# The edge stage of a graph attention as one block, its wide lookups in three pairs of PSUM banks, and its first step and key decoding placed earlier

## The reference, cut to what matters

```python
def _forward(x, edge_index, W_gat, att_src, att_dst, b_gat, ...):
    h = (x_flat @ W_gat).reshape(M, HEADS, NUM_EXPERTS)      # 4 heads, 4 experts
    loops = jnp.arange(M)
    src = jnp.concatenate([edge_index[0], loops])            # 524288 edges
    dst = jnp.concatenate([edge_index[1], loops])
    a_src, a_dst = (h * att_src).sum(-1), (h * att_dst).sum(-1)
    e = jax.nn.leaky_relu(a_src[src] + a_dst[dst], negative_slope=0.2)
    e_max = jax.ops.segment_max(e, dst, num_segments=M)
    ee = jnp.exp(e - e_max[dst])
    denom = jax.ops.segment_sum(ee, dst, num_segments=M)
    alpha = ee / (denom[dst] + 1e-16)
    msg = h[src] * alpha[:, :, None]
    agg = jax.ops.segment_sum(msg, dst, num_segments=M).reshape(M, 16) + b_gat
```

## Time and profile before

| what | us |
|---|---|
| median of 3 runs | 1919.39 |
| the runs | 1917.76 to 1920.73 |
| the profiled execution, its own time | 1920.45 |
| its span | 1918.7 |
| start of the table block's work (VectorE L1036) | 705.72 |
| first tail lookup selected (L1433) | 736.56 |
| first block of the main loop (L1345) | 838.41 |
| end of the main loop | 1226 |

### The profile page before, as it was taken

How to read it: one execution, slowest core, us unless ns; L and a number is a source line. 1 busy time by engine, 2 the same in 40 slices (tenths; PEclk the granted TensorE clock), 3 DMA queues, 4 the chain that set the end, 5 groups by cost and what they waited for, 6 DMA issues and landing times. The chain is left out here.

```text
span 1918.7 us, 32883 instructions
## 1 busy us (share of the span) xinstructions
PE 1447.2 (75%) x11347; PEld 1094.5 (57%) x11347; DVE 1321.2 (69%) x2871; ACT 850.4 (44%) x2486; POOL 774.4 (40%) x712
## 2 busy tenths in 40 slices
PE   0005205999999935978888878899998689699998
PEld 0005204888888724756666656557777555357777
DVE  7989976888888746768888866666645334565544
ACT  2402724999999942024444411644431322553331
POOL 0268745666666426737677775000000000560000
PEclk9999999999999977988888888989999699899999
DMA  9000000000000011000000010032222641144454
GB/s 352 14 2 3 1 0 2 1 0 0 0 0 0 0 38 8 9 5 9 8 8 7 8 9 5 2 112 89 79 100 83 151 89 33 23 162 156 151 180 154
DMA packets 74008, 98.35 MB, mean 51 GB/s; under 512 B 17680, under 2 KB 62144, under 8 KB 67648
## 3 DMA queue, kind: packets, MB, share of 16 engines
q1 hardware_dynamic: 53600, 88.77, 13.7%
q0 software_dynamic: 9984, 3.21, 2.1%
q10 hardware_dynamic: 10336, 5.25, 1.4%
HBM read 83.23 MB, written 13.84 MB: 51 GB/s over the span
## 5 line engine op out<-in xcount | busy, mean ns | idle before, releaser
L1163 POOL DMA_INDIRECT sb_ge_gs<-source_rows,sb_ge_idx x288 | 284.7, 989 | 132.2 <-issue 85.4
L1895 ACT ACTIVATE sb_x_ht<-x_pu,sb_x_b 128x512 f32<-128x512 f32 x256 | 175.1, 687 | 239.7 <-PE x_pu L1905 239.5
L1925 PEld LDWEIGHTS x_py<-sb_x_w,sb_x_ht 128*128 128x128 f32 x2048 | 245.8, 193 | 45.7 <-issue 35.0
L1925 PE MATMUL x_py<-sb_x_w,sb_x_ht 128*128 128x128 f32 x2048 | 254.9, 279 | 4.2 <-DVE sb_x_ht L1967 3.2
L1905 PE MATMUL x_pu<-sb_TT,sb_x_w 128*128 128x512 f32 x512 | 243.9, 608 | 8.0 <-ACT sb_x_ht L1895 5.0
L1561 PE MATMUL acc<-sb_ge_b,sb_ge_ol 128*128 128x320 f32 x576 | 200.9, 487 | 56.2 <-DVE sb_ge_b L1345 56.2
L201 POOL TENSOR_TENSOR sb_bias<-sb_PB,sb_TT 128x1024 f32<-128x1024 f32 x64 | 151.4, 2366 | 123.2 <-DVE sb_logits L244 123.2
L281 ACT ACTIVATE sb_probs<-sb_logits,sb_neg_max 128x128 f32<-128x128 f32 x512 | 197.8, 399 | 0.0
L1967 DVE TENSOR_TENSOR sb_x_ht<-sb_x_ht,sb_x_wide 128x512 f32<-128x512 f32 x256 | 164.6, 686 | 4.6 <-DMA sb_x_wide<-gate_rows 3.8
L1561 PEld LDWEIGHTS acc<-sb_ge_b,sb_ge_ol 128*128 128x128 f32 x576 | 112.3, 211 | 96.2 <-DVE sb_ge_b L1345 62.5
L1209 ACT ACTIVATE sb_ge_olt<-p_turned 128x512 f32<-128x512 f32 x72 | 43.0, 597 | 270.6 <-PE p_turned L1538 270.6
(11 more groups left out here) (403 smaller groups left out, 3220.1 us busy)
## 6 DMA issues: line engine op xcount, KB each, us to landing
sb_x_wide<-gate_rows SPq DMA_DIRECT2D x45, 1024.0 KB, 7.0
sb_ge_gs<-source_rows,sb_ge_idx POOLq DMA_INDIRECT x288, 2.3
sb_z<-in_L_conv_z SPq DMA_DIRECT2D x1, 4096.0 KB, 20.2
sb_TT<-in_L_conv_mask SPq DMA_DIRECT2D x1, 4096.0 KB, 42.6
normed_rows<-sb_TT SPq DMA_DIRECT2D x4, 1024.0 KB, 6.9
sb_mr_xg<-normed_rows SPq DMA_DIRECT2D x32, 128.0 KB, 2.6
sb_X<-x_rows ACTq DMA_DIRECT2D x8, 512.0 KB, 11.3
x_rows<-sb_X SPq DMA_DIRECT2D x3, 1024.0 KB, 5.6
```

The lines of the kernel that those rows point to most:

```text
L1163: pool.indirect_dma_start(GS[:, j, k, :], None, SRC_T, bass.IndirectOffsetOnAxis(ap=IDX[:, j, k:k + 1], axis=0))\
L1895: nc.scalar.activation(HT[:, g % SLOTS, c, :], PU[n % NU][:, :], ACT.Gelu, bias=bb1[:, c:c + 1]).then_inc(hidden, 1)
L1925: last = nc.tensor.matmul(PY[k][:, 0:C], HT[:, g % SLOTS, c, k * P:(k + 1) * P], w2[:, c, :], start=False, stop=(c == NCH - 1))
```

## The change

The tables become part of the edge block, so there is one block where there were two:

- The largest source term over the partitions is found with a turn on TensorE, a VectorE maximum over the turned row, a 4x4 diagonal and a second matmul that spreads it over the partitions. POOL's `partition_all_reduce` is gone. The scratch for it lies in `B`, and `sb_ge_b` is the name of that buffer in the listings.
- The tail's keys are decoded while TensorE does this. POOL can start the tail gathers when these and the store of the rows are done. SyncE loads the keys first, then stores the rows.
- The tail's low one-hots come in three pieces of 8 columns, each with its own count of `t_hot`, in an order of slots (`t_slot`) in which the slots of step 0 come free first.
- The lookups of the tail use `LOOK`, `ACC[0:2]` and `ACC[2:4]` in turn, and so wait only for the select three groups before. `ACC` is cleared behind the last select.
- `count_rest` stands behind the first 16 tail blocks on VectorE, and its matmuls behind them on TensorE.
- Three of the four one-hots of the steps 0 and 1 are made between the last tail blocks; TensorE runs the turns and lookups of step 0 between the last tail blocks.
- Keys are decoded four steps ahead of their use in place of three.

```diff
+        t_look = lambda g: (LOOK[:, :, :], ACC[:, 0:2, :], ACC[:, 2:4, :])[g % 3]
+        TOP_ALL = TURNED[:, 2 * P:2 * P + GHEADS]
+        t_slot = lambda k: k + STEP if k < SLOT else k - SLOT if k < STEP else k + SLOT
...
             for u in range(2):
                 load(0, u, True)
+            sp.wait_ge(rows_in, 1)
+            sp.dma_start(SRC_T.rearrange("(r s) w -> r s w", r=P), HS[:, :, :]).then_inc(rows_stored, 16)
...
-            n_both, n_gather, n_rest = counts(pool)
             pool.wait_ge(t_decoded, 1)
             pool.wait_ge(rows_stored, 16)
             for k in range(TAIL):
                 pool.indirect_dma_start(GST[:, k, :], None, SRC_T, bass.IndirectOffsetOnAxis(ap=IDXT[:, k:k + 1], axis=0))\
...
+            n_both, n_gather, n_rest = counts(pool)
...
-            self_terms(OWN, GT[:, :, 0:8], H[:, :, :])
+            pool.wait_ge(tables_made, 1)
+            self_terms(OWN, GT[:, :, 0:8], H)
...
+            act.wait_ge(tab_args, 1)
+            nc.scalar.activation(GT[:, :, 0:4], S, ACT.Exp)
+            nc.scalar.activation(GT[:, :, 4:8], S, ACT.Exp, scale=0.2)
...
+            act.wait_ge(tab_args, 2)
+            nc.scalar.activation(GT[:, :, 8:12], LOW, ACT.Exp)
+            nc.scalar.activation(GT[:, :, 12:16], M, ACT.Exp).then_inc(tables_made, 1)
...
             for u, (k0, k1) in enumerate(PARTS):
...
+                if u == 0:
+                    with act.Fori(0, n_rest) as i:
+                        act.wait_ge(c_digits, i + 1)
+                        low_hots(i, 0)
...
+            link = Chain(v, tab_chain)
+            nc.vector.memset(ones, 1.0)
+            link(nc.vector.tensor_reduce(TOP, S.rearrange("p s h -> p h s"), AX.X, ALU.max))
+            v.sem_inc(topped, 1)
+            key_bits = TAILK[:, :].bitcast(I32)
+            nc.vector.tensor_scalar(BY_ROW[:, 0, :], key_bits, P - 1, NODE_BITS - LO_BITS, ALU.bitwise_and, ALU.logical_shift_left)
+            nc.vector.tensor_scalar(BY_ROW[:, 1, :], key_bits, LO_BITS, TILES - 1, ALU.logical_shift_right, ALU.bitwise_and).then_inc(parted, 1)
+            v.wait_ge(parted, 1)
+            nc.vector.tensor_tensor(IDXT[:, :], BY_ROW[:, 0, :], BY_ROW[:, 1, :], ALU.bitwise_or).then_inc(t_decoded, 1)
+            nc.vector.tensor_scalar(LOT[:, :], key_bits, NODE_BITS, P - 1, ALU.logical_shift_right, ALU.bitwise_and)
+            nc.vector.tensor_scalar(HIT[:, :], key_bits, NODE_BITS + LO_BITS, (VALID >> 20) + TILES - 1,
+                                    ALU.logical_shift_right, ALU.bitwise_and).then_inc(t_decoded, 1)
+            v.wait_ge(top_turned, 1)
+            link(nc.vector.tensor_reduce(TOPT, TURNED[0:GHEADS, 0:P], AX.X, ALU.max))
+            link(nc.vector.tensor_scalar(diagonal, ident[0:GHEADS, 0:GHEADS], TOPT, None, ALU.mult))
+            v.sem_inc(diagonal_made, 1)
...
+            v.wait_ge(top_spread, 1)
+            top = TOP_ALL.unsqueeze(1).to_broadcast([P, TILES, GHEADS])
+            link(nc.vector.tensor_tensor(S, S, top, ALU.subtract))
+            v.sem_inc(rows_in, 1)
+            v.sem_inc(tab_args, 1)
+            link(nc.vector.tensor_tensor(TARGETS, TARGETS, top, ALU.add))
+            v.sem_inc(targets_made, 1)
...
-                        numbers_of(t, j + 3)
+                    if c == 1 and ahead >= 4:
+                        decode(t, j + 4)
+                    if c == 2 and ahead >= 4:
+                        numbers_of(t, j + 4)
...
-            nc.vector.tensor_tensor(OLT_IN[:, 0:TAIL, :], NUMBERS.unsqueeze(1).to_broadcast([P, TAIL, P]),
-                                    LOT[:, :].unsqueeze(2).to_broadcast([P, TAIL, P]), ALU.is_equal).then_inc(t_hot, 1)
+            for k in range(0, TAIL, SLOT):
+                nc.vector.tensor_tensor(OLT_IN[:, t_slot(k):t_slot(k) + SLOT, :], NUMBERS.unsqueeze(1).to_broadcast([P, SLOT, P]),
+                                        LOT[:, k:k + SLOT].unsqueeze(2).to_broadcast([P, SLOT, P]), ALU.is_equal).then_inc(t_hot, 1)
...
-            for j in range(3):
+            link(nc.vector.scalar_tensor_tensor(out=M, in0=TARGETS, scalar=0.2, in1=TARGETS, op0=ALU.mult, op1=ALU.max))
+            link(nc.vector.tensor_tensor(LOW, TARGETS, M, ALU.subtract))
+            link(nc.vector.scalar_tensor_tensor(out=M, in0=TARGETS, scalar=0.2, in1=M, op0=ALU.mult, op1=ALU.subtract))
+            v.sem_inc(tab_args, 1)
+            for j in range(4):
                 decode(0, j)
...
+            n_both, n_gather, n_rest = counts(v)
...
+                nc.vector.tensor_tensor(sel, t_look(g).rearrange("p b (k h x) -> p (b k) h x", h=GHEADS, x=TILES),
                                         OHT[:, k, :].unsqueeze(2).to_broadcast(shape), ALU.mult).then_inc(t_selected, 1)
...
+            def count_rest():
...
+                v.wait_ge(hot_made, n_rest * CPS)
+
...
+                if u == 0:
+                    v.wait_ge(tables_made, 1)
                 for k in range(k0, k1):
                     if k >= NB:
                         v.wait_ge(t_b_free, k - NB + 1)
                     nc.vector.tensor_tensor(B[:, k % NB, :, :, :].rearrange("p k x w -> p (k x) w"),
                                             OHT[:, k, :].unsqueeze(2).to_broadcast([P, TILES, PART]),
                                             MSG[:, k - k0, :].unsqueeze(1).to_broadcast([P, TILES, PART]), ALU.mult).then_inc(t_b_made, 1)
+                    if k >= STEP + NB - 1 and k - STEP - NB + 1 < 3:
+                        v.wait_ge(t_b_free, STEP)
+                        one_hots(0, (k - STEP - NB + 1) // 2, (k - STEP - NB + 1) % 2)
+                if u == 0:
+                    count_rest()
...
             select(0, 0)
             weigh(0, 0)
             count_bits(n_rest * UNIT + FIRST_N, n_rest)
             v.wait_ge(act_hot, n_rest + AHEAD)
             count_digits(n_rest, 0)
             message(0, 0)
+            v.wait_ge(t_b_free, TAIL)
+            one_hots(0, 1, 1)
...
-                left = OL[:, :, :, :].rearrange("p u k l -> p (u k) l")[:, k, :]
+                left = OL[:, :, :, :].rearrange("p u k l -> p (u k) l")[:, t_slot(k), :]
...
-                if g > 0:
-                    pe.wait_ge(t_selected, g)
+                if g >= 3:
+                    pe.wait_ge(t_selected, g - 2)
...
+                    last = nc.tensor.matmul(t_look(g)[:, k // 2, at:at + GHEADS * TILES], OLT[:, g % CHUNKS, k * P:(k + 1) * P],
...
+            pe.wait_ge(topped, 1)
+            nc.tensor.transpose(TURNED[0:GHEADS, 0:P], TOP, ident[:, :]).then_inc(top_turned, 1)
+            pe.wait_ge(diagonal_made, 1)
+            nc.tensor.matmul(TOP_ALL, ones, diagonal, start=True, stop=True).then_inc(top_spread, 1)
+            n_both, n_gather, n_rest = counts(pe)
+            pe.wait_ge(targets_made, 1)
             turn_tail(0)
             for g in range(TAIL // CHUNK):
                 if g + 1 < TAIL // CHUNK:
                     turn_tail(g + 1)
                 look_tail(g)
+            pe.wait_ge(t_selected, TAIL // CHUNK)
+            for q in range(QUARTERS):
+                nc.tensor.matmul(ACC[:, q, :], zero, zeros, start=True, stop=False, skip_group_check=True)
+            for k in range(STEP):
+                scatter_tail(k)
             with pe.Fori(0, n_rest) as i:
                 for c in range(CPS):
...
-            for k in range(TAIL):
+            for k in range(STEP, TAIL):
                 scatter_tail(k)
...
-                look(0, 0, c)
...
+                c = k - (TAIL - CHUNKS - 2)
+                if 1 <= c <= CHUNKS:
+                    look(0, 0, c - 1)
+                if 0 <= c < CHUNKS + 2:
+                    turn(0, c // CHUNKS, c % CHUNKS)
```

123 lines of the change are left out of this document (29 added, 94 removed).

## The result

The changed kernel takes 1887.61 us as a median of 4 runs (1884.48 to 1888.91), the kernel before 1918.58 beside it (1915.19 to 1920.73). The ratio is 0.9838, with a 95% interval of 0.9818 to 0.9857: 31.0 us less, 27 to 35 by the interval. The profiled execution took 1887.2, its span is 1885.4.

What follows compares the result with a forecast made beforehand. Before the loop, engines waiting for each other; in it, TensorE and VectorE set the pace. The loop's first block moves from 838.41 to 805.9, 32.5 gained, loop unchanged: 1920.45 − 32.5 = 1888.0 profiled, 1887 median, range 1884.5 to 1889.5.

Steps and rivals of the forecast that it cites:

- S − top: Head: subtraction of the maximum starts at 708.5, not 712.16, with the new maximum taking 2.1 us for POOL's 5.76 us wait.
- the loop: Main loop: length unchanged at 387.6 us, bounds −5 and +1.
- The head: Up to the first select: select at 721.6 behind ScalarE's chain, in place of 736.56, 15.0 us gained.
- the block's end and start vanish: Head: before, M was done at 715.38 and useful tail work came at 726.00; now VectorE's work follows in a row.
- trip counts: Head, VectorE: 1.50 us, to 721.3, hidden with the fourth decoding by ScalarE's chain by 0.3 us only.
- The rival of POOL's own wait: Head: POOL's first instruction comes as late as the all-reduce did, all following 3.9 us later, 1891; chance 0.05.
- The gathers: Tail: sixteen gathers from 712.0, last landing at 735.0, needed at 736.6, so hidden by 1.6 us.
- The clears: Behind the last select: 3.9 to 5.4 us, ending 739.3 to 740.7, costing 0 to 0.4.
- the rival of the clock: TensorE stays at 1.2 GHz through some groups, the clears and a few blocks: costs 2 to 6, 1889 to 1893; chance 0.16.
- The three pairs: Six wide groups: VectorE sets a period of 2.50 in place of 3.37, last sum ends at 736.6, 19.3 gained so far.
- the counts: Behind 16 tail blocks: cost 3.6 us of idle TensorE, given back of the 6.6 gained by moving them.
- The term for step 0: Between the last tail blocks, TensorE: seven blocks, four turns and four lookups take 20.2 us, to 798.8.

Runs made afterwards that it cites:

- copies first: Changed kernel with three decodings moved behind tail blocks 4 to 6, and ScalarE copying two groups of turned one-hots before the last four exponentials: 1886.72 us, one run.
- step 0 after the blocks: Changed kernel with step 0's one-hots, turns and lookups back behind all 24 tail blocks: 1900.64 us, ratio 0.9897 to the kernel before.
- three steps ahead: Changed kernel with keys decoded three steps ahead in place of four: 1887.17 us, ratio 0.9834 to the kernel before.
- clears early and warm: Changed kernel with bank pairs in another turn, accumulators cleared as they come free, and ten clears in place of four: 1888.15 us, ratio 0.9848 to the kernel before.
- clears early: Changed kernel with bank pairs in another turn and accumulators cleared after the fourth and fifth select: 1888.19 us, ratio 0.9847 to the kernel before.

## Why the prediction was right, step by step

The forecast was 1887 and 1887.61 came. The way there was as worked out, but that the two numbers are this close is in part luck: the gain was forecast as 32.5 us and is 31.0, the kernel before was 0.8 lower this time, and the terms below miss in both directions. Positions are given from the copy, as predicted (less 704.72) and as measured (less 703.72).

| step | predicted | measured |
|---|---|---|
| S − top | 3.8 | 4.2 |
| first tail gather | 7.3 | 9.4 |
| ScalarE's first copy | 11.6 | 12.0 |
| first select | 16.9 | 16.7 |
| select to select | 2.50 | 2.61 |
| last sum ends | 31.9 | 32.2 |
| first tail block, VectorE | 34.1 | 34.4 |
| its matmuls | 35.8 | 37.3 |
| TensorE idle or counting ahead of block 16 | 3.6 | 3.6 |
| step 0's select | 94.3 | 95.9 |
| first block of the loop | 101.2 | 102.6 |
| the loop | 387.6 | 388.6 |

**The head: right size, and its cause only half told.** 15.2 us came where 15.0 were forecast. The prediction put 3.6 on the all-reduce itself and the rest on the block's border, the trip counts and the order. The kernel before with TensorE's maximum alone moves its first select from 31.8 to 21.0, so 10.9 of the 15.2 hang on the all-reduce in the old layout: 3.7 directly, and 7.2 because POOL's numbers had come late behind it. The rows stood there: 14.72 of idle for "issue" ahead of the all-reduce, 11.33 ahead of the numbers. The step "the block's end and start vanish" took the second for the border's price. The sum held since both edits go together. The four kernels put the first select at 31.8 (before), 21.0 (TensorE's maximum alone), 19.8 (one block with POOL's all-reduce) and 16.7 (both): the border with the order and the trip counts is worth 12.0 with the all-reduce and 4.3 without, and no run takes these three apart. The 1.50 us of trip counts on VectorE never showed: with the copies first, the select follows the high one-hots after 0.17. From ScalarE's first copy, 0.4 late, to the select were 4.7 us and not 5.2, and so the select came 0.2 sooner than said. The rival of POOL's own wait did not come: its numbers are at 704.68.

**The gathers: the margin was 1.6 us, and it was used up.** The first gather is 2.1 later than said. The store started 0.4 later and took 3.8 to land and not 2.9, and POOL's first gather came 0.9 behind SyncE's load, which waits for the same store. That 0.9 is there in all twelve kernels with one block and stays open; the store's time differs between executions of the same code, 2.9 in seven of them and 3.8 to 4.8 in five. VectorE waited 0.32. With the same order and a store of 2.9 (step 0 after the blocks, three steps ahead, clears early and warm) it waited for no gather, and its first block is where it is here, at 34.3 to 34.9. The first messages took 1.9 in place of 2.25 to the block, which paid for it.

**The clears: mis-sized.** The term was 0 to 0.4, with the clears at 3.9 to 5.4; they took 6.2, at a clock of 0.56 behind 4 us of idle TensorE, and cost 1.4. That is the rival of the clock, at its smallest. By the early and the warm clears the choice was between this and 1.8 of slow first blocks.

**The three pairs, the counts, step 0.** The sixfold period was taken at 2.50 and is 2.61: VectorE keeps 0.03 to 0.14 between its instructions. Taken back one at a time the parts are worth 3.9 (banks), 3.9 (counts) and 10.2 (step 0). The term for step 0, 7 blocks and 4 of each piece in 20.2, was 20.3 (778.97 to 798.43 and 0.84). The counts came as worked out: 3.6 us of TensorE without blocks. Decoding four steps ahead is worth nothing, as said.

**The total.** The stretch gained 31.1 and not 32.5, the loop gave back 1.2: 1918.58 − 31.1 + 1.2 = 1888.7. The measured median lies 1.1 under that. In the two profiled executions what follows the loop differs by 2.4 us, with the same code, so 1.1 is inside what the code outside the change varies by.

## What to carry to other kernels

An engine's idle time for "issue" ahead of a cheap instruction can belong to that instruction's kind, and come again at the next ordinary one, wherever in the kernel that stands: one all-reduce on POOL was paid for twice in both layouts, and a small maximum by a turn and a matmul cost 2 us in its place. Small TensorE pieces that wait on other engines are worth putting between long matmuls: here they were hidden, and the clock stayed up. And when a stretch ahead of a loop gets shorter, look at what in the loop goes by another engine's clockwork (here POOL's last gathers and self terms): of 6 us gained ahead of it, 3.35 went because the loop met that work in a worse place, and the rest went too.

## What the runs showed of the hardware that was not expected

- POOL's all-reduce of 0.39 us has 5.99 us of idle time ahead of it (5.3 to 5.5 behind its operand) that no instruction explains, and one more such wait follows at the next ordinary instruction of POOL, 7.03 us where that came over 400 us later. Gathers in between did not pay.
- A VectorE tensor_tensor of 0.42 us took 1.88 beside a POOL tensor_tensor, in which both read two SBUF operands.
- In the kernel with clears early, after 5.5 us without work TensorE's first four microseconds of matmuls ran at 0.51 of the clock, 1.2 GHz, and the next four at 1.00; with ten clears in place of four ahead of them they ran at 1.00 from the first. Counted from the first select, the added zeros paid 1.8 us.
- Of the loop's first thirteen distances from select to select, those with a mean granted clock of 0.92 are 21.6 to 21.8 us and those with 0.85 or 0.86 are 22.1 to 24.3, and which steps are which shifts with the loop's start. That a loop's length can differ by a microsecond or so for that alone is not shown.
